# Offset convolution on tiles of 64 rows by 32 columns for each image, instead of 96 rows by 64 columns for two images

## The reference

```
om  = conv3x3(x, w_off) + b_off          # 27 channels: 9 y offsets, 9 x offsets, 9 mask logits
for each pixel and each of the 9 taps:   # bilinear sample at (y + ky + off_y, x + kx + off_x)
    s[tap] = sigmoid(mask[tap]) * bilinear(x, py, px)
out = relu(batchnorm(sum over taps and channels of w * s + b)) + x
```

## Time and profile before

| | us |
|---|---|
| median of 3 runs | 861.25 (858.91 to 863.65) |
| span of the profiled execution | 859.9 |
| shifted copies issued by SP | 224.3 to 257.1 |
| PE in `offsets`, first to last start | 239.0 to 303.2 |
| x offsets loaded back, first issue | 312.1 |

### The profile page before, as it was taken

How to read it: one execution, slowest core, us unless ns; L and a number is a source line. 1 busy time by engine, 2 the same in 40 slices (tenths; PEclk the granted TensorE clock), 3 DMA queues, 4 the chain that set the end, 5 groups by cost and what they waited for, 6 DMA issues and landing times.

```text
span 859.9 us, 30275 instructions
## 1 busy us (share of the span) xinstructions
PE 692.2 (80%) x12282; PEld 500.2 (58%) x12282; DVE 719.1 (84%) x935; ACT 584.7 (68%) x1089; POOL 603.3 (70%) x401
## 2 busy tenths in 40 slices
PE   5968888885999958888888788888878887777763
PEld 1325565554446647666766666667666666555542
DVE  3469999997322119999999999999999999999975
ACT  2646776774213239788788798888888988777714
POOL 3047888781410008898898998999999999989960
PEclk9989999998999979999999999999999999999976
DMA  4000000000481148555555555565466555555302
GB/s 164 1 0 2 1 0 0 0 0 0 112 204 27 21 106 207 140 156 151 141 140 162 145 158 147 143 166 161 120 167 166 141 157 152 160 146 156 96 4 98
DMA packets 29937, 90.69 MB, mean 105 GB/s; under 512 B 10622, under 2 KB 10750, under 8 KB 29566
## 3 DMA queue, kind: packets, MB, share of 16 engines
q1 hardware_dynamic: 26672, 88.12, 38.3%
q10 hardware_dynamic: 3150, 0.88, 0.5%
HBM read 79.01 MB, written 3.28 MB: 96 GB/s over the span
## 4 chain that ended last, share of the span: by engine, by line
PE 40%; DVE 39%; issue 15%; ACT 2%; DMA 1%; POOL 1%; DVEq 1%; ACTq 0%; SPq 0%; POOLq 0%
PE PS L1128 40%; DVE region L767 19%; DVE region L779 9%; DVE region L645 2%; DVE region L601 2%; DVE region L605 1%; DVE region L620 1%; DVE region L607 1%; PE PS L1210 1%; DVE region L602 1%; DMA region<-px_scratch 1%; ACT region L874 0%; DVE region L575 0%; DVE region L561 0%; DMA cst<-in_consts 0%
## 5 line engine op out<-in xcount | busy, mean ns | idle before, releaser
L1128 PE MATMUL PS<-region 64*64 64x144 f32 (+3 forms) x10112 | 456.4, 292 | 112.6 <-issue 81.2
L1128 PEld LDWEIGHTS PS<-region 64*64 64x64 f32 (+1 forms) x10112 | 342.2, 134 | 219.9 <-issue 198.3
L767 DVE TENSOR_TENSOR region<-PS,region 128x864 f32<-128x864 f32 x384 | 381.2, 1046 | 12.4 <-PE PS L1128 12.3
L509 POOL TENSOR_TENSOR region<-region 128x768 f32<-128x768 f32 x128 | 202.4, 1581 | 67.5 <-DVE region L767 67.5
L513 POOL TENSOR_TENSOR region<-region 128x864 f32<-128x864 f32 x128 | 224.0, 1750 | 18.7 <-POOL region L509 0.4
L1006 ACT ACTIVATE region<-region 128x1152 f32<-128x1152 f32 x128 | 149.2, 1165 | 34.3 <-PE PS L1128 30.6
L1003 ACT ACTIVATE region<-region,cst 128x1152 f32<-128x1152 f32 x128 | 159.2, 1244 | 7.7 <-DMA region<-px_scratch 6.3
L779 DVE TENSOR_REDUCE region<-region 128x32 f32<-128x960 f32 x128 | 145.9, 1140 | 1.5 <-POOL region L513 1.5
L1037 ACT ACTIVATE region<-x,cst (+2 forms) x288 | 86.7, 414 | 0.0
L1128 PE MATMUL PS<-wg,xp 64*64 64x144 f32 x1024 | 82.6, 286 | 5.0 <-issue 4.9
L432 POOL TENSOR_TENSOR region<-region,cst 128x1024 f32<-128x1024 f32 x32 | 61.4, 1917 | 31.4 <-PE PS L1203 25.3
(11 more groups left out here) (118 smaller groups left out, 590.6 us busy)
## 6 DMA issues: line engine op xcount, KB each, us to landing
region<-px_scratch SPq DMA_DIRECT2D x256, 288.0 KB, 4.3
out<-region SPq DMA_DIRECT2D x4, 512.0 KB, 3.0
region<-xp SPq DMA_DIRECT2D x8, 140.2 KB, 2.9
region<-xp SPq DMA_DIRECT2D x8, 140.1 KB, 2.8
region<-xp SPq DMA_DIRECT2D x8, 140.0 KB, 2.9
cst<-in_consts SPq DMA_DIRECT2D x1, 1104.0 KB, 8.6
region<-xp SPq DMA_DIRECT2D x8, 132.0 KB, 2.7
region<-xp SPq DMA_DIRECT2D x8, 131.9 KB, 2.7
```

What stands on the lines that cost most here:

```text
L509: pool.tensor_tensor(two_rows[:, :, :, 0:2 * THIRD - KEEP], two_rows[:, :, :, 0:2 * THIRD - KEEP], two_rows[:, :, :, KEEP:2 * THIRD], ALU. ...
L767: v.tensor_tensor(uu[:, 2 * u:2 * u + 2, :, THIRD * t:THIRD * (t + 1)], PS[:, 2 * t:2 * t + 2, 0:THIRD * C].rearrange("p h (a o) -> p h o ...
L1128: return nc.tensor.matmul(o, l, r, start=start, stop=stop)
```

## The change

A tile of TensorE now holds one image instead of two. The 16 channels of an image and its 3 shifts take 48 partitions (0 to 47 for images 0 to 3, 64 to 111 for images 4 to 7), and its 27 channels take 32 columns. The 4 images of a half stand beside each other on the 128 output partitions, and both halves of the array are used. `offsets` has 24 matmuls a chunk (3 ky, 4 images g, 2 halves h), of 48 rows by 32 columns. The shifted copies are made for each image: 96 DMAs of 16 partitions instead of 48 of 32. `woff` is 32 columns wide and is built by three instructions that depend on each other. `bcol` is filled by four DMAs.

```diff
-    place = np.concatenate([[W * (g // 2) + OC * (g % 2) + k for k in range(OC)] for g in range(PAIRS)])
+    place = np.concatenate([[32 * g + k for k in range(OC)] for g in range(PAIRS)])
...
-        woff = sb("woff", [P, 3, W])
+        woff = sb("woff", [P, 3, 32])
...
-                row = W * (g // 2) + OC * (g % 2) + KK
+                row = 32 * g + KK
...
-                for g in range(PAIRS):
+                for g in range(B):
                     for kx in range(3):
                         a, b = (W + 2) * edges[j], (W + 2) * edges[j + 1] - kx
-                        sp.dma_start(xs_of(g)[32 * kx:32 * (kx + 1), a:b], xp[32 * g:32 * (g + 1), a + kx:b + kx]).then_inc(xs_in[j], 16)
+                        at = W * (g // PAIRS) + C * kx
+                        sp.dma_start(xs_of(g % PAIRS)[at:at + C, a:b], xp[C * g:C * (g + 1), a + kx:b + kx]).then_inc(xs_in[j], 16)
...
+            wk = w_("woff").rearrange("p (t x k) -> p t x k", t=3, k=OC)
             for kx in range(3):
-                part, e = slice(32 * kx, 32 * (kx + 1)), 2 * (kx % 2)
-                v.tensor_tensor(
-                    woff[part, :, 0:2 * OC].rearrange("p t (b k) -> p t b k", b=2),
...
+                if kx == 0:
+                    ins = v.tensor_scalar(woff[:, :, 0:OC], wk[:, :, kx, :], c_("bmod")[:, 0:1], None, ALU.mult)
+                else:
+                    dve.wait_ge(woff_ready, kx)
+                    ins = v.scalar_tensor_tensor(woff[:, :, 0:OC], wk[:, :, kx, :], c_("bmod")[:, kx:kx + 1], woff[:, :, 0:OC], ALU.mult, ALU.add)
+                ins.then_inc(woff_ready, 1)
...
-            for half in range(2):
-                act.dma_start(bcol[W * half:W * half + 2 * OC, :], boff[2 * OC * half:2 * OC * (half + 1), :]).then_inc(b_in, 16)
+            for g in range(PAIRS):
+                act.dma_start(bcol[32 * g:32 * g + OC, :], boff[OC * g:OC * (g + 1), :]).then_inc(b_in, 16)
...
-                for h in range(2):
-                    for ky in range(3):
-                        for side in range(2):
-                            ins = mm(PS[W * side:W * (side + 1), 2 * h + u, :], woff[0:96, ky, :],
-                                     grid(xs_of(2 * h + side), W + 2)[0:96, n * RPC + ky:n * RPC + ky + RPC, 0:W], start=ky == 0, stop=ky == 2)
-                    ins.then_inc(om_ready, 1)
+                for ky in range(3):
+                    for g in range(PAIRS):
+                        for h in range(2):
+                            part = slice(W * h, W * h + 3 * C)
+                            ins = mm(PS[32 * g:32 * (g + 1), 2 * h + u, :], woff[part, ky, :],
+                                     grid(xs_of(g), W + 2)[part, n * RPC + ky:n * RPC + ky + RPC, 0:W], start=ky == 0, stop=ky == 2)
+                            if ky == 2 and g == PAIRS - 1:
+                                ins.then_inc(om_ready, 1)
...
-                    pe.wait_ge(xs_in[(n + 1) // 2], 16 * 3 * PAIRS)
+                    pe.wait_ge(xs_in[(n + 1) // 2], 16 * 3 * B)
```

More of the change, by code:

```diff
@@ L418, in _ @@
             pool.tensor_tensor(wg[:, :, :], mid(w_("w"), PAIRS), end(c_("bmod"), KK * C), ALU.mult).then_inc(wg_ready, 1)
-            pool.wait_ge(b_in, 32)
+            pool.wait_ge(b_in, 16 * PAIRS)
             pool.tensor_tensor(bcol[:, :], bcol[:, :], c_("kxadd"), ALU.add).then_inc(wb_ready, 1)
@@ L705, in _ @@
             dve.wait_ge(woff_zero, 2)
+            wk = w_("woff").rearrange("p (t x k) -> p t x k", t=3, k=OC)
             for kx in range(3):
-                part, e = slice(32 * kx, 32 * (kx + 1)), 2 * (kx % 2)
-                v.tensor_tensor(
-                    woff[part, :, 0:2 * OC].rearrange("p t (b k) -> p t b k", b=2),
-                    w_("woff")[part].rearrange("p (t x k) -> p t x k", t=3, k=OC)[:, :, kx, :].unsqueeze(2).to_broadcast([32, 3, 2, OC]),
-                    mid(c_("bmod")[part, e:e + 2], 3).unsqueeze(3).to_broadcast([32, 3, 2, OC]), ALU.mult).then_inc(woff_ready, 1)
+                if kx == 0:
[4 more added lines that the diff above has]
+                ins.then_inc(woff_ready, 1)
             dve.wait_ge(eca_back, 1)
```

## The result

The changed kernel takes 878.53 us (median of 4 runs, 877.31 to 880.49), the kernel before 861.62 beside it: a ratio of 1.0188, 95% interval 1.0153 to 1.0223. It is slower by 16.9 us. The forecast was 877, with 860 to 886 as its range, and +16.1 as the shift. (The 861.25 that it started from is the median of three of the four runs behind 861.62.)

The account below looks back on a forecast made before the run. PE bounds the serial offset stage; after the change SP's 96 copies delay the first store, so `to_samples(6)` ends at 323.6 instead of 307.5. 861.25 + 16.1 gave 877 us, range 860 to 886 (the forecast's own 871 to 884).

Parts of the forecast that it names:

- Eight tiles at once: `offsets` on PE: eight 64x32 tiles run together, 2.58 us a chunk instead of 5.15; the period falls from 9.05 to 6.48.
- 0.634 us a copy, whatever its size: Shifted copies on SP's queue: 96 issues at 0.634 us each plus long issues, ending at 289.8 instead of 257.1.
- L754 of chunk 2 at 292.8: DVE's addition (L751 in the prediction) waits for the first store behind the copies, 289.8 + 3.0, and ends at 294.2.
- `to_samples(2)` at 294.2: PE, idle for some 11 us, starts `to_samples(2)` when DVE's addition for chunk 2 ends, at 294.2.
- the sum: Offset stage: `to_samples(6)` ends at 323.6 instead of 307.5, a shift of +16.1 us, so 877 us for the kernel.
- Two us for the clock: PE after its pause runs at a granted clock of 0.50 for some 3.8 us, which loses 2 us.
- The tail unchanged: End of the offset stage: last stores, their landing and the loads back take the same on both sides.
- cheap small copies: Rival on SP's queue: copies of 16 partitions cost less to issue; 841 to 850 us (0.13), or about 861 (0.10).
- tiles that don't run at once: Rival on PE's `offsets`: with four tiles at a time 887 us, with two 908; chance 0.07.
- the 18 to 20 that the rivals had: Gains in rivals: -18 us (843) if issue waits for DMA engines, 20.6 (841) if PE alone counts; 841 to 850 had 0.13.

Follow-up runs that it names:

- the first three experiments: Kernel before with 96 copies of 16 partitions: 888.27 us; changed kernel with five bands of rows: 894.78 us; changed kernel with all stores on ACT's queue: 864.98 us.
- the last two: Changed kernel with eleven groups of 4 DMAs issued by SP after its last output: 944.72 us; changed kernel with twelve single stores there instead: 901.87 us.
- the probe: Changed kernel, with SP issuing eleven groups of 4 DMAs of various shapes and directions after its last output has landed: 944.72 us.
- the last experiment: Changed kernel, with SP issuing twelve single stores of 9 partitions after its last output, each when the one before has landed: 901.87 us.
- the run that broke the order: Changed kernel with its 96 copies on SP, ACT and GpSimd, GpSimd not waiting for band 2 before band 3: 862.59 us, ratio 1.0021.
- the three kernels with old tiles: Kernel before: 861.62 us; the same with 96 copies of 16 partitions: 888.27 us; the same with its 48 copies spread over three queues: 862.14 us.

## Why the prediction was right

- **Eight tiles at once** (2.58 us a chunk): right. An `offsets` went from 5.30 us (253.17 to 258.47) to 2.73 (268.37 to 271.10, and the same for chunks 5 to 7; chunk 4, right after the pause, took 3.08), which is the 2.57 forecast. The period became 6.64, not 6.48: the 0.16 is all in `to_samples`, which takes 1.69 us to the next `offsets` (266.68 to 268.37) instead of 1.53.
- **0.634 us a copy, whatever its size**: right in size. The last issue ended at 289.7, as forecast, from two errors that cancel: the copies began 1.5 us later (below), and the long issues cost 3.1 us in all, not 4.7. The prediction doubled them with the number of copies; in the traces they lie where something else runs. Each of the 18 shifted copies that took over 1 us to issue in the seven kernels that copy on SP's queue alone (the kernel before, the changed one, the first three experiments and the last two) lies at a 16 KB packet of the `instruction` queue, as 1.71 us from 241.46 and the packet at 241.60 before, and 1.84 from 267.09 and the packet at 267.19 after. The reason that the prediction drew from the Trainium skill's rule ("DMA: Bandwidth & Descriptors", on the increment by 16) was not borne out: the rule says how many engines share a transfer, and by it copies of 8 and 9 partitions go to 8 and 9 engines, but the probe shows them dearer than 16 to issue. The row that the prediction took as agreeing, a store at 0.326 beside a copy at 0.592, differs also in direction and shape. The cheap rows have DRAM on one side, but so have the loads back at 0.596.
- **L754 of chunk 2 at 292.8**: 292.75.
- **`to_samples(2)` at 294.2**: wrong, 297.81. The prediction let PE finish `first(2)` beforehand, and put ACT at nothing, since its 2.9 us of work fit in a period; it is ACT's place in the order that costs, not its work. The third round of `first(2)` needs a PSUM bank that ACT empties, and ACT stands in its own stream at the wait for chunk 2's L754, with four stores to issue before that: 3.65 us that the sum didn't have.
- **Two us for the clock**: 1.6 in `to_samples(2)` (3.13 instead of 1.53) and 0.35 in `offsets(4)`: right. About 0.5 more is in the round of `first(2)` before, and is part of the 3.65.
- **The tail unchanged**: not quite. From the end of `to_samples(6)` to the first load back it is 3.0 us instead of 4.65, since the last store landed in 1.55 instead of 3.22 us; the last experiment says what lay beside it.
- The sum: `to_samples(6)` ends at 327.7 and not 323.6 (+3.65 for ACT, +0.5 for longer periods), the tail takes 1.65 back, and 16.1 + 4.1 - 1.65 = 18.5, which is the shift in the trace (the span, 876.0 in the sum, is 878.7). 1.5 us of it lie ahead of the change: in this execution matmuls near 15 us lasted 2.08 us a pair and not 1.12 (the profile gives the granted clock as 1.00 in both, so the cause isn't shown), and every later row stands 1.5 us later. The first copy starts anywhere from 223.0 to 228.3 in the eleven profiles, with old tiles and new. That leaves 17.0 beside the medians' 16.9. So the ACT step was missed, and the tail and chance hid it partly: that the total came out within 1 us of the forecast shift is in part luck.
- **The rivals**: cheap small copies fell with the first row read, and tiles that don't run at once with the 2.73 us of an `offsets`. The other half of the cheap copies' case, that the small tiles win once the issue is out of the way, was sound: with three queues in the order of need the change is faster than before by 0.8%, but by 7 us and not the 18 to 20 that the rivals had. What holds it there is still mostly the issue on SP: `offsets(1)` starts when the 36th copy on SP's queue has landed, 24.9 us from the first issue to that one's and 3.0 to its landing, and 35 spacings of 0.634 are 22.2 of the 24.9. ACT's half of band 1 had landed by 247.1, over 5 us before. A spreading that gives SP fewer of the first 36 copies wasn't run.

## What to carry to other kernels

Before a tile is made smaller, count the DMAs that feed it: an issue has a price for each instruction that halving its bytes doesn't halve, and what stands behind them on the same queue pays first. When an engine is busy all through a stage, look at what its speed was hiding; the row to read was DVE's wait for a store, 5.57 us that nobody felt. When a wait comes loose, follow every engine's stream past it, also the one that empties the banks (here ACT). And when copies are spread over queues, issue them in the order in which they are needed, for the DMA engines are shared: their share was 1.0 in the run that broke the order.

## What the hardware showed that was not expected

- The price of a plain copy's issue on SP follows the direction: 0.59 us SBUF to SBUF with 16 partitions, 0.41 to 0.45 from or to DRAM with 16 or 128. The kernel's loads back from DRAM cost 0.57 to 0.60 all the same, with idle DMA engines. GpSimd issued the copies of 16 partitions in 0.484 us.
- 9 partitions SBUF to SBUF took 0.742 us to issue, 8 took 0.656: more than 16.
- 48 matmul records of 48x32 tiles start eight at a time, each 0.43 us, the step that two at a time took with 96x64.
- A 16 KB packet of the `instruction` queue, 0.9 to 1.4 us long, lies at each of those 18 issues above 1 us, and inside the landing of the last store in the three kernels with old tiles (3.22, 3.29 and 3.05 us), but in none of the kernels with new ones (1.55 to 1.59 us). It was seen, not tested.
